# Graph attention with residual and layer norm on one core: sum and reciprocal moved to GpSimd, more compares on VectorE

## Reference

```python
h = einsum('bnf,hfo->bhno', x, W)                 # 8 x 8 heads x 2048 x 64
s1 = einsum('bhno,ho->bhn', h, a1); s2 = einsum('bhno,ho->bhn', h, a2)
e = leaky_relu(s1[..., :, None] + s2[..., None, :], 0.2)
attn = softmax(where(adj > 0, e, -9e15), axis=-1)  # per head 2048 x 2048
h_prime = einsum('bhnm,bhmo->bhno', attn, h)       # heads joined: N x 512
x = layernorm(x + h_prime)                         # eps 1e-5, over the features
```

## Time and profile before

| | us |
|---|---|
| median of 3 runs | 2871.23 (2862.51 to 2875.33) |
| the profiled execution's own time | 2872.58 |
| its span in the profile | 2870.6 |
| TensorE busy | 2669.8 (93%) |
| VectorE busy | 2510.0 (87%) |
| ScalarE busy | 2337.4 (81%) |
| GpSimd busy | 1077.6 (38%) |
| granted TensorE clock, mean | 0.978 |

### The profile page before, as it was taken

The page is one execution under the profiler, slowest core; times in us unless marked ns, Lnnn a source line. Parts: engine busy times, 40 slices in busy tenths (PEclk is TensorE's granted clock), DMA queues, the critical chain, the costliest instruction groups (busy, mean ns, idle before and its releaser), DMA issues.

```text
span 2870.6 us, 126143 instructions
## 1 busy us (share of the span) xinstructions
PE 2669.8 (93%) x52546; PEld 2317.7 (81%) x52546; DVE 2510.0 (87%) x3828; ACT 2337.4 (81%) x3894; POOL 1077.6 (38%) x1011
## 2 busy tenths in 40 slices
PE   6999999999999899999999999899998999899996
PEld 3699867988589895898949998499984998759986
DVE  6898978999789988899888998889988999889996
ACT  3699974999669994799938998399983999839995
POOL 4633335333343324433253332633326233263332
PEclk9999999999999999999999999999999999999998
DMA  6467652676527754377543775447744577445773
GB/s 177 119 132 175 150 141 72 142 173 143 142 65 165 175 137 117 72 177 169 136 104 87 176 164 128 118 93 174 165 120 120 111 173 150 124 105 126 175 150 99
DMA packets 281206, 390.20 MB, mean 136 GB/s; under 512 B 161857, under 2 KB 161857, under 8 KB 280673
## 3 DMA queue, kind: packets, MB, share of 16 engines
q1 hardware_dynamic: 253536, 315.24, 41.4%
q0 software_dynamic: 27136, 67.12, 15.0%
HBM read 313.52 MB, written 34.14 MB: 121 GB/s over the span
## 4 chain that ended last, share of the span: by engine, by line
ACT 36%; PE 28%; DVE 16%; issue 13%; DMA 3%; POOL 1%; DVEq 0%; ACTq 0%; SPq 0%; POOLq 0%
ACT m_pos L607 33%; PE ps L530 10%; PE ps L499 5%; PE ps L561 5%; PE ps L562 5%; DMA y<-in_x 3%; DVE m_neg L832 3%; ACT adj_cut L573 2%; DVE m_pos L825 2%; DVE prod L796 2%; ACT xT L579 1%; DVE prod_d L799 1%; DVE m_pos L811 1%; DVE b_both L794 1%; PE ps L435 1%
## 5 line engine op out<-in xcount | busy, mean ns | idle before, releaser
L607 ACT ACTIVATE m_pos<-ps,s_steep 128x512 fp8e4<-128x512 f32 x3440 | 2092.7, 1068 | 354.0 <-PE ps L449 302.8
L530 PE MATMUL ps<-b_both,m_pos 128*128 128x130 f16 x16384 | 1019.4, 221 | 80.3 <-DVE total L670 52.0
L561 PE MATMUL ps<-d_hi,m_neg 128*128 128x65 f16 x16384 | 1039.1, 194 | 20.6 <-issue 20.2
L562 PE MATMUL ps<-d_lo,m_neg 128*128 128x65 f16 x16384 | 1038.7, 194 | 7.1 <-issue 6.7
L562 PEld LDWEIGHTS ps<-d_lo,m_neg 128*128 128x128 fp8e5 x16384 | 1010.3, 98 | 38.8 <-issue 25.4
L530 PEld LDWEIGHTS ps<-b_both,m_pos 128*128 128x128 fp8e5 x16384 | 964.2, 98 | 92.5 <-issue 91.4
L561 PEld LDWEIGHTS ps<-d_hi,m_neg 128*128 128x128 fp8e5 x16384 | 1019.7, 98 | 17.6 <-issue 17.2
L825 DVE TENSOR_TENSOR m_pos<-m_pos,maskT 128x1024 uint32<-128x1024 uint32 x512 | 633.0, 1255 | 156.1 <-ACT m_pos L607 140.0
L991 POOL TENSOR_TENSOR den_scaled<-den_inv,bound 128x4 f32<-128x4 f32 x256 | 251.3, 982 | 1260.5 <-DVE den_inv L681 1204.0
L832 DVE TENSOR_TENSOR m_neg<-m_pos,maskT 128x2048 uint32<-128x2048 uint32 x256 | 583.8, 2280 | 0.3
L499 PE MATMUL ps<-W_sb,xT 128*128 128x512 f32 x1024 | 461.7, 612 | 45.3 <-DVE prod_d L799 43.4
(11 more groups left out here) (94 smaller groups left out, 1552.3 us busy)
## 6 DMA issues: line engine op xcount, KB each, us to landing
adj_in<-in_adj SPq DMA_DIRECT2D x266, 512.0 KB, 4.8
s_bc<-s_rows SPq DMA_DIRECT2D x258, 256.0 KB, 3.6
x_in<-in_x SPq DMA_DIRECT2D x134, 256.0 KB, 4.1
x_sum<-in_x POOLq DMA_DIRECT2D x128, 256.0 KB, 4.8
y<-in_x POOLq DMA_DIRECT2D x32, 1024.0 KB, 11.0
out<-y SPq DMA_DIRECT2D x32, 1024.0 KB, 7.4
maskT<-adj_cut SPq DMA_TRANSPOSE x264, 3.9
m_neg<-in_x SPq DMA_DIRECT2D x10, 256.0 KB, 3.7
```

The costliest lines, as they stand in the source:

```text
L530: mm = pe.matmul(acc, mask, b_both[:, j, h, :, :], start=(j == 0 and it % 2 == 0), stop=(j == JC - 1 and it % 2 == 1))
L561: pe.matmul(acc, mask, d_hi[:, j, h, :], start=(j == 0), stop=False)
L562: mm = pe.matmul(acc, mask, d_lo[:, j, h, :], start=False, stop=(j == JC - 1))
L607: ins = nc.scalar.activation(chunk(m_pos[h % 2], j, 0, BLK), ps[:, BANK_S1 + h % 2, :], ACT.Relu, bias=s2_steep[:, j, h:h + 1], scale=STEE ...
```

## The change

- GpSimd, at the head of `divide_unit`, adds total and neg_part, raises column 64 to the power of -1 (into the new tile `den`), and goes on as before. VectorE's `take_neg` ends with neg_part, which is now double. GpSimd waits for take_pos and for neg_part; VectorE waits for neg_read once at the start of a batch.
- DVE_SLOTS: 1, 2 and 3 compares of a unit become 2, 3 and 4. The units with the middle value move by one with the normalisation and are one fewer, so that by the code's rule a batch has 115 where it had 82.
- The three parts of the normalisation, deviation and the store stand at heads 2, 3, 4, 4 and 6 instead of 1, 2, 3, 3 and 5. The split stage keeps its places.

```diff
--- before.py
+++ after.py
@@ -41,7 +41,7 @@
 BLK = 512
 QUADS = 2
 
-DVE_SLOTS = {1: {0: (7,), 1: ()}, 2: {0: (7,), 1: (7,)}, 3: {0: (6, 7), 1: (7,)}}
+DVE_SLOTS = {1: {0: (7,), 1: (7,)}, 2: {0: (6, 7), 1: (7,)}, 3: {0: (6, 7), 1: (6, 7)}}
 
 
 
@@ -82,7 +82,7 @@
         k, h = divmod((unit - 2) % UNITS, H)
         if unit in (0, 1) or k * H + h == STAT_UNIT:
             return DVE_SLOTS[1]
-        if (k and h in (2, 3)) or k * H + h in (0, STAT_UNIT + 1):
+        if (k and h in (3, 4)) or k * H + h in (0, STAT_UNIT + 1):
             return DVE_SLOTS[2]
         return DVE_SLOTS[3]
 
@@ -179,9 +179,10 @@
         mean_part = sb("mean_part", [P, H, O1], F16)
         mean_next = sb("mean_next", [P, H, O1], F16)
         mean = sb("mean", [P, H, O1], F16)
-        neg_part = sb("neg_part", [P, IT, O1], F32)
+        neg_part = [sb(f"neg_part{i}", [P, IT, O1], F32) for i in range(2)]
         total = [sb(f"total{i}", [P, IT, O1], F32) for i in range(2)]
-        den_inv = [sb(f"den_inv{i}", [P, IT], F32) for i in range(2)]
+        den = [sb(f"den{i}", [P, IT], F32) for i in range(2)]
+        minus_one = sb("minus_one", [P, IT], F32)
         den_scaled = [sb(f"den_scaled{i}", [P, IT], F32) for i in range(2)]
         ln_stats = sb("ln_stats", [P, IT, 6], F32)
         ln_mv = sb("ln_mv", [P, IT, 2], F32)
@@ -395,7 +396,7 @@
                                 load_x(JC * (b + 1) + t, t % 2, ((b + 1) * (JC // 2) + t // 2) % (NBLK * IT // 2))
                         if unit == STURN_UNIT + 1:
                             store_s1(b + 1)
-                        if h == 5:
+                        if h == 6:
                             if k:
                                 store_block(g - 1, (k - 1) % 2)
             store_block(NBLK - 1, 1)
@@ -674,11 +675,8 @@
                 r = r_row[:, it0:it0 + IT, h:h + 1].to_broadcast([P, IT, O1])
                 dve.wait_ge(unit_done, at(unit_done, u + 1))
                 neg = ps[:, 2 + hp, 0:IT * O1].rearrange("p (t c) -> p t c", t=IT)
-                V.tensor_tensor(neg_part[:], neg, r, ALU.mult).then_inc(neg_read, 1)
-                dve.wait_ge(neg_read, at(neg_read, u + 1))
-                V.tensor_tensor(total[hp][:], total[hp][:], neg_part[:], ALU.add).then_inc(total_made, 1)
-                dve.wait_ge(total_made, u + 1)
-                V.reciprocal(den_inv[hp][:], total[hp][:, :, O]).then_inc(den_inverted, 1)
+
+                V.tensor_tensor(neg_part[hp][:], neg, r, ALU.mult).then_inc(neg_read, 1)
 
             def ln_first_half(g, par):
                 dve.wait_ge(y_made, 16 * (g + 1))
@@ -768,6 +766,8 @@
                 dve.wait_ge(s2_turned, n + 1)
 
             def batch_start(b):
+                dve.wait_ge(neg_read, at(neg_read, UNITS * b))
+                dve.sem_inc(waited[dve.engine], 1)
                 dve.wait_ge(exp_made, b + 1)
                 V.tensor_copy(r_row[:], r_next[:]).then_inc(r_row_made, 1)
                 V.tensor_scalar(k_b[:], e_b[:], kappa[:, 0:1], None, ALU.mult)
@@ -938,7 +938,7 @@
                             no_edge(b + 1)
                             turn_s2(b + 1)
                             dve.sem_inc(waited[dve.engine], 1)
-                        for when, work in ((1, ln_first_half), (2, ln_statistics), (3, ln_apply)):
+                        for when, work in ((2, ln_first_half), (3, ln_statistics), (4, ln_apply)):
                             if h == when and k:
                                 work(g - 1, (k - 1) % 2)
                         if unit < UNITS - 2:
@@ -987,8 +987,14 @@
 
             def divide_unit(u, h, g, par):
                 hp = h % 2
+                pool.wait_ge(pos_read, at(pos_read, u + 1))
+                pool.sem_inc(waited[pool.engine], 1)
+                pool.wait_ge(neg_read, at(neg_read, u + 1))
+                G.tensor_tensor(total[hp][:], total[hp][:], neg_part[hp][:], ALU.add).then_inc(total_made, 1)
+                pool.wait_ge(total_made, u + 1)
+                G.tensor_tensor(den[hp][:], total[hp][:, :, O], minus_one[:], ALU.pow).then_inc(den_inverted, 1)
                 pool.wait_ge(den_inverted, u + 1)
-                G.tensor_tensor(den_scaled[hp][:], den_inv[hp][:], bound[:].to_broadcast([P, IT]), ALU.mult
+                G.tensor_tensor(den_scaled[hp][:], den[hp][:], bound[:].to_broadcast([P, IT]), ALU.mult
                                 ).then_inc(den_made, 1)
                 if h == 0:
                     pool.wait_ge(out_stored, at(out_stored, 16 * (g - 1)))
@@ -1005,6 +1011,7 @@
 
             G.memset(ones[:], 1.0)
             G.memset(minus_half[:], -0.5)
+            G.memset(minus_one[:], -1.0)
             G.memset(x_sum[:], 0.0)
             G.memset(ident[:], 0.0).then_inc(ident_step, 1)
             pool.wait_ge(ident_step, 1)
@@ -1048,7 +1055,7 @@
                             add_x(JC * b + t, t, t % 2, ((b + 1) * (JC // 2) + t // 2) % (NBLK * IT // 2))
                         if unit == XSUM_UNIT + 1:
                             clear_x_sum(b + 1)
-                        if h == 3 and k:
+                        if h == 4 and k:
                             deviation(g - 1)
                         if h == 0 and k:
                             residual(g - 1, (k - 1) % 2)
```

## The result

The changed kernel takes 2846.17 us (median of 15 runs) against 2865.18 for the kernel before beside it: ratio 0.9941, interval 0.9928 to 0.9954, so 0.6% faster. The forecast was 2813 from 2871, 2.0%. The direction and the range held, the size was more than three times too large. The profiled execution took 2860.0 us, its span is 2855.7.

What follows compares the result with a forecast made beforehand. No single engine: TensorE bounds block 0, ScalarE blocks 1 and 2. Per batch 3.8 + 1.0 + 1.4 + 1.4, times 8, less 1.4 and 1.2, saves 58 us: 2813 us from 2871; range 2780 to 2864.

Steps and rivals of the forecast that it cites:

- The chain's 6.9 us: GpSimd's longer chain per head, held up by every mask product: 6.9 us, against about 2.7 before.
- The move's own worth: Normalisation a head later removes VectorE's waits for the residual DMA in blocks 2 and 3: 1.4 us a batch.
- Rival (a): Running power holds the shared port, delaying VectorE's XOR product L832; about 8 us a batch slower, 2935 us; chance 0.12.
- 3.4 us in three blocks of eight batches: Blocks 1 to 3: GpSimd's add collides with back-to-back mask products, costing VectorE 0.42 us a head, 3.4 us a block.
- the 47 us a run for compares and GpSimd's part together: Share of the 58 us forecast saving from moved compares, add and reciprocal, without the normalisation's move.
- 6.1 us a batch saved: Block 2 to the next batch's start: 2.3 in block 2, 1.0 in block 3, 1.4 at turn, 1.4 by move.
- GpSimd is far from full.: GpSimd has room for a chain of about 2.8 us a head alone, against about 0.9 before.
- The residual starts at most 4 us later: Blocks 2 and 3: the longer GpSimd chain delays the residual DMA by at most 4 us; a head is 8 us.
- All 12 waits go.: With normalisation a head later, VectorE's 12 residual waits outside the tail vanish, about 2.7 us each.
- rival (b): GpSimd late after the residual, L670 waiting for the y product, 2 us in three blocks: 2862 us, no change; chance 0.08.
- No gain, the add's collision eats what was moved.: VectorE in blocks 1 and 2: 3.2 us added, 5.3 saved, 3.4 lost to collision, giving 68.1 and 68.5 us.
- Rival (c): Only the batch turn and DMA waits are won, blocks 1 and 2 stay at 71 us: 2842 us; chance 0.20.

Runs made afterwards that it cites:

- e7: Kernel before with only the normalisation a head later (82 compares, add and reciprocal on VectorE): 2851.2 us, ratio 0.9950.
- e3: Kernel before with 115 compares and the normalisation a head later, add and reciprocal still on VectorE: 2851.9 us, ratio 0.9946.
- e2: Changed kernel with the earlier 82 compares a batch instead of 115: 2864.4 us, ratio 0.9982 to the kernel before.
- e9: Changed kernel with add and reciprocal back on VectorE in units 28 and 29 only: 2835.8 us, ratio 0.9903 to the kernel before.
- e10: Changed kernel with the residual DMA issued ahead of the x_sum DMA at head 0: 2836.6 us, ratio 0.9905 to the kernel before.
- e12: Changed kernel with the add back on VectorE, only the inversion (power) on GpSimd: 2821.9 us, ratio 0.9865 to the kernel before.
- e18: e12 plus a spare 128x260 add on GpSimd before the power, its result unread: 2891.1 us, ratio 1.0086 to the kernel before.
- e13: e12 with the residual DMA issued ahead of the x_sum DMA: 2838.0 us, ratio 0.9904 to the kernel before.
- e14: e12 with 82 compares on VectorE instead of 115: 2863.5 us, ratio 0.9985 to the kernel before.
- e15: Kernel before with only add and inversion moved to GpSimd (82 compares, normalisation at its earlier heads): 2875.7 us, ratio 1.0038.
- e5: Changed kernel with a copy in place of GpSimd's partition_all_reduce, leaving out the maximum over partitions: 2827.8 us, ratio 0.9868 to the kernel before.

## Why the prediction was wrong

*Right.* The compares are 115 a batch, as counted (920 in the run). ScalarE was the bound of blocks 1 and 2 and stopped being it at the cost worked out. Block 1 came to 69.7 us, the forecast's own number, though from 72.0 and not 71.2. VectorE's net there was nothing, as said: it is busy for 67.5 us of units 8 to 16, where it was busy for 67.2. The chain's 6.9 us was right (1605.62 to 1612.40 in the rows of the collision), and so was the 1.2 us that the tail grew by (from the last batch's unit 31 to the end 22.2 us before, 23.3 after). The move's own worth was put at 1.4 us a batch, 11 us; e7 has 14, though mostly in block 3 and not in block 2 where most of the waits were. Rival (a) did not come: the XOR product was not held back by a running power.

*Right by luck.* The add collides with the mask products where the earlier trace rows said, and the 71 us by which VectorE's work got longer are near the 82 that 3.4 us in three blocks of eight batches make. But the mask products have only 24 of them. The forecast had every pair of those blocks collide and took nothing for L832 and the compares; in fact 75 pairs collided, L832 took 24 us more and the compares about 30.

*The step that failed* is the 47 us a run for compares and GpSimd's part together (the 58 less the move's 11). After against e7 it measures 0.1%, with overlapping intervals: nothing. On top of the move, the compares alone are worth nothing (e3), and GpSimd's part alone costs 0.3% (e2). By stages, blocks 0 and 1 gained more than forecast (0.5 and 2.3 us against 0 and 1.5). From unit 16 to the next batch's unit 0 the forecast had 6.1 us a batch saved (2.3 in block 2, 1.0 in block 3, 1.4 at the turn, 1.4 by the move); measured, 0.5 were lost (210.6 to 211.1). The sentences of the prediction that this part rests on, and what the runs show in place of each:

- "GpSimd is far from full." It is at 68%, but it was late at two places, and the forecast put that at nothing. The first is the reduction in units 28 and 29. The earlier trace rows say how short a head was then; no row that I chose showed the gap of over 15 us, though the trace of before has it. Units 27 to 31 took 1.7 us more where I had 1.0 less, and the turn 0.3 less where I had 1.4. TensorE's longest wait for the first chunk did fall as forecast (6.0 to 4.8 us), but ScalarE's wait for s_neg grew from 46.3 to 67.1 us, 3 us in each of seven turns. With add and reciprocal back on VectorE in these two units (e9) 1.0 of the 1.7 and 0.4% of the time come back.
- "The residual starts at most 4 us later" and "All 12 waits go." It starts 6 to 8 us later (e10). The longer chain makes GpSimd come to the x_sum DMA 4.5 us later, 7.8 us after neg_part of unit 15 and not 3.3, and the residual stands behind that DMA in GpSimd's queue for the rest. Five waits stayed and block 2 gained 1.0 us and not 2.3. With the residual first (e10) the waits are gone and 0.4% is won, if only just clear of noise. This is close to rival (b), GpSimd late, which had a chance of 0.08 and the x_sum DMA behind the residual instead of ahead of it; its sign, waits of L670 (now L671) for the y product, came in units 18 and 30.
- "No gain, the add's collision eats what was moved." For VectorE's busy time this was so. But the add also made GpSimd's chain longer, and that has a price: e12 against after shows 0.8%, 22 us, for having the add on GpSimd, all of it from unit 16 on, none in blocks 0 and 1. That e9 and e10 give 0.4% each fits, but they were not run together. e18 prices the add on GpSimd without any relief of VectorE at 70 us; the relief gave most of it back (after is 1.4% faster than e18).

Rival (c), 2842, said almost the time, for half the reason: the move pays. Its ground that blocks 1 and 2 stay at 71 was wrong, since block 1 gained and the turn did not. The prediction's sign of being wrong, blocks 1 and 2 above 71 us, came true in batch 5 (71.8 and 72.5), but not in the mean (69.7 and 70.5).

*What stays open.* One thing is the 0.4% between e12 and e13. Another is why the compares are worth 1.2% with the power on GpSimd (e14 against e12) and nothing without it (e3 against e7). The traces give a part: in units 8 to 16 ScalarE is full in e7 (71.9 of 72.0 us) and in e14 (72.2 of 72.3). With the compares moved, VectorE is the busiest in e3 (69.7 of 71.8 us, ScalarE 69.3), while in e12 it is at 68.1 of 69.9. So without the power on GpSimd the compares seem to hand the bound from ScalarE to VectorE. That the reciprocal's 0.18 us and its wait, all that differs on VectorE, are enough for it was not tested.

## What to carry to other kernels

When three engines are within 5% of each other, ask at each stage which one is full: here the relief of another engine paid nothing (e2, e15). The two moves have to be priced together, stage by stage: 33 compares were worth 1.2% in one version of this kernel, nothing in a second, and cost 1.9% in a third.

Before lengthening a chain on a lightly loaded engine, read that engine's own longest gaps and its DMA queue: its share of busy time says nothing on when it is late. Here the gaps were in the trace of before.

Of two steps that could move to GpSimd, move the one that touches little memory (the inversion of four values) and leave the one that reads two full tiles: 1.4% against 0.6% here.

Look at the granted clock and at several batches before taking one as typical: the batch used here had a clock fall in the changed kernel that seven of eight did not have in that block.

## What was not expected of the hardware

- A GpSimd operation on four values per partition is as exposed as a large one: the power took 1.02 to 3.76 us (median 1.90) and the small product 0.20 to 2.31, waiting beside VectorE's two-operand instructions. The Trainium skill, "SBUF — State Buffer", "Who interferes with whom", has this as an exclusive lock on a shared port pair; the trace agrees for GpSimd's waiting. But the power, once begun, held up nothing on VectorE: 89 XOR products in the changed kernel and the second mask product of 162 pairs in e12 began under a running power at their usual length. So it does not behave as a holder for its whole length.
- One partition_all_reduce a batch kept GpSimd away for over 15 us with 0.74 us of it visible. About 3 us of that are the wait for its input; the rest stands behind the MODIFY_POOL_CONFIG ahead of it and the one after it. Taking it out gained 0.7% (e5).
